# Expert layer: 0/1 products on TensorE turn slots into tokens; rows gathered and results scattered block by block

## The chip, the cores and the metric

The kernel runs on one core of a Trainium2 chip. The metric is device time in microseconds (us). A core has TensorE (matmuls), VectorE, ScalarE and GpSimd (called DVE, ACT and POOL in the profile), and SyncE (SP). SP and ACT issue plain DMAs, GpSimd the indirect ones, whose addresses come from a table in SBUF.

## The reference

A decoder of two layers on x [2, 1024, 256] (2048 tokens of 256 values). The change lies in the mixture of experts that ends the first layer:

```python
moe_in = _layer_norm(x_resid, ln2_g, ln2_b)
xf = moe_in.reshape(N, D)
probs = jax.nn.softmax(xf @ w_gate, axis=-1)
top_w, top_i = jax.lax.top_k(probs, TOP_K)
top_w = top_w / top_w.sum(-1, keepdims=True)
for e in range(E):
    gate_e = jnp.sum(jnp.where(top_i == e, top_w, 0.0), axis=-1)
    he = jax.nn.gelu(xf @ w1[e] + b1[e])
    out = out + gate_e[:, None] * (he @ w2[e] + b2[e])
return out.reshape(B, S, D) + x_resid
```

N is 2048 tokens, D 256, the hidden width F 1024, E 8 experts, TOP_K 2. Everything is float32.

## The kernel before

Stages follow each other, each a block of five instruction streams with a barrier between blocks: mixers, cross attention, self attention, `norm`, `experts`, and then the second layer. Activations stay in SBUF with the 256 features on partitions (h, res, x: 128 partitions x 2 x 2048 tokens).

`experts` doesn't run all tokens through all experts. Each token has two chosen experts, so there are 4096 (token, choice) pairs. They are sorted into slots: each expert owns whole blocks of NSL = 256 slots, and NB = 23 blocks hold any distribution (5888 slots).

**Routing.** SP loads seven small tables (L2118). TensorE makes the logits, 16 tiles of 128 tokens, 8 columns each (L2154), then transposes h into rows of tokens (L2161), which ScalarE copies to `ht` (L2360). VectorE takes the softmax and ranks the experts of a token by comparing all pairs (L2267 to L2271), TensorE counts ahead of each token (L2167, L2168), and VectorE turns the counts into `owner` (L2291: the expert of each block, which lets SP and ACT load the first weights, L2122 and L2353) and `place` (L2300: the slot of each token's choices).

**Dispatch.** GpSimd scatters the rows of `ht` to their slots in a DRAM tensor `moe_in_rows` that SP filled with zeros during the norm, 16 tiles x 2 choices (L2384). SP waits for all 32 and loads the first blocks of 256 rows (L2126).

**Loop over the blocks b.** TensorE turns a block's rows back to columns (`turn`, L2183), multiplies by w1 (`first`, L2194), ScalarE applies gelu (L2371), TensorE multiplies by w2 (`second`, L2206). VectorE copies the turned columns (`keep_columns`, L2314) and the results (`keep_rows`, L2321). SP loads rows and w1 two blocks ahead and stores results to `moe_out_rows` (L2132); ACT loads w2. The order on TensorE is written out by hand:

```python
for b in range(NB):
    if b + 1 < NB:
        first(b + 1)
    if b + 2 < NB:
        turn(b + 2)
    second(b)
```

**End.** GpSimd gathers each token's two result rows tile by tile into a ring of 8 (L2392). For each tile VectorE forms share0 x row0 + bias (L2336) and adds share1 x row1 (L2340), TensorE turns the sum (L2237), and after every fourth tile VectorE adds it to x (L2347). The bias products are TensorE's too (L2226). VectorE adds res to x beforehand (L2308).

## Time and profile before

| | us |
|---|---|
| median of 3 runs (2878.31 to 2885.4) | 2885.22 |
| the profiled execution, its own time | 2872.27 |
| its span | 2870.4 |
| TensorE busy in the span | 2411.5 (84%) |
| VectorE busy | 1872.3 (65%) |
| GpSimd busy | 1530.5 (53%) |
| ScalarE busy | 1301.5 (45%) |

The profile is one execution, with times from the start of its span. Busy shares are means over stages with different limits, so the part around the change has to be read by itself: `norm` ends at 1614.0 and the expert stage runs from there to 2090.3, about 476 us. The granted clock is TensorE's, as a share of 2.4 GHz; it has two levels, 0.5 (1.2 GHz) and 1.0. A float32 matmul stands as two records.

### The profile page before, as it was taken

How to read it: one execution, taken by the hardware profiler on the slowest of the kernel's cores; microseconds unless marked ns; L12 is line 12 of the kernel's file. 1: busy time of each engine (PE TensorE's matmuls, PEld its weight loads, DVE VectorE, ACT ScalarE, POOL GpSimd, SP SyncE). 2: the span in 40 equal slices, each digit the busy share in tenths (PEclk: the TensorE clock that was granted, in tenths of full speed). 3: DMA queues.
4: the chain of work that ended last, by engine and by line, in shares of the span. 5: the costliest groups of instructions: out<-in, count | busy, mean ns of one | idle time of the engine just before them, and what ended most of it. 6: DMA issues, size and time to landing. Idle time of an engine off the chain costs nothing. (4 is left out here: it accounts for less than half of the span.)

```text
span 2870.4 us, 26873 instructions
## 1 busy us (share of the span) xinstructions
PE 2411.5 (84%) x8432; PEld 1100.3 (38%) x8432; DVE 1872.3 (65%) x2521; ACT 1301.5 (45%) x2063; POOL 1530.5 (53%) x1340
## 2 busy tenths in 40 slices
PE   7989889899897778678888539999788899787868
PEld 3333323333332233333333328888533333223322
DVE  2999999999999933466653400000229999996334
ACT  4556566465664434345555202222045564543433
POOL 2999999999999811500000140000339999994110
PEclk9999999999999999899999669999789999999989
DMA  5031230312303000612310334444340312300000
GB/s 189 2 117 40 101 123 1 125 54 73 118 1 117 0 22 17 145 23 33 46 23 1 103 128 183 176 173 170 109 166 3 117 45 74 118 0 21 1 9 30
DMA packets 72484, 215.18 MB, mean 75 GB/s; under 512 B 14331, under 2 KB 39558, under 8 KB 53782
## 3 DMA queue, kind: packets, MB, share of 16 engines
q1 hardware_dynamic: 65668, 180.85, 19.4%
q10 hardware_dynamic: 3602, 24.22, 2.6%
q0 software_dynamic: 3072, 8.39, 0.9%
q8 instruction: 68, 1.11, 0.2%
q14 instruction: 74, 0.61, 0.1%
HBM read 187.80 MB, written 25.43 MB: 74 GB/s over the span
## 5 line engine op out<-in xcount | busy, mean ns | idle before, releaser
L897 POOL TENSOR_TENSOR s_dbu<-s_dx,s_bc 128x512 f32<-128x512 f32 x768 | 966.9, 1282 | 35.0 <-DVE s_psum L561 31.5
L480 PE MATMUL s_psum<-s_hc,ident 128*128 128x512 f32 x1536 | 834.6, 634 | 168.3 <-DVE s_hc L581 145.6
L764 ACT ACTIVATE s_psum<-s_dt,s_a_neg 128x512 f32<-128x512 f32 x768 | 521.6, 688 | 606.6 <-DVE s_hc L581 605.6
L480 PEld LDWEIGHTS s_psum<-s_hc,ident 128*128 128x128 f32 x1536 | 258.9, 193 | 684.6 <-DVE s_hc L581 479.5
L581 DVE TENSOR_TENSOR s_hc<-s_psum,s_bc 128x512 f32<-128x512 f32 x624 | 419.8, 673 | 0.6 <-PE s_psum L480 0.4
L561 DVE TENSOR_TENSOR_SCAN s_psum<-s_psum,s_state,s_dbu 128x512 f32<-128x512 f32 x312 | 395.2, 1278 | 10.9 <-POOL s_dbu L897 7.2
L561 DVE TENSOR_TENSOR_SCAN s_psum<-s_psum,s_dbu 128x512 f32<-128x512 f32 x312 | 381.3, 1222 | 14.3 <-POOL s_dbu L897 11.9
L1979 ACT ACTIVATE s_probs<-s_banks 128x512 f32<-128x512 f32 (+3 forms) x384 | 169.7, 493 | 148.6 <-PE s_banks L1704 105.8
L2392 POOL DMA_INDIRECT s_rows_in<-moe_out_rows,s_place x32 | 30.8, 963 | 358.5 <-DMA moe_out_rows<-s_ys 349.1
L2371 ACT ACTIVATE s_hidden<-s_banks,s_w 128x256 f32<-128x256 f32 x184 | 77.1, 470 | 302.5 <-PE s_banks L2194 302.5
L163 POOL TENSOR_TENSOR s_pair<-s_res 128x512 f32<-128x512 f32 x4 | 5.0, 1269 | 384.5 <-issue 383.1
L432 PE MATMUL s_psum<-s_pad,s_taps 128*128 128x512 f32 x384 | 191.2, 592 | 0.0
L908 POOL TENSOR_TENSOR s_hc<-s_hs,s_bc 128x512 f32<-128x512 f32 x144 | 182.8, 1269 | 15.4 <-DVE s_hs L561 15.4
L1828 DVE TENSOR_REDUCE s_umax<-s_banks 128x1 f32<-128x512 f32 (+3 forms) x256 | 138.8, 585 | 69.7 <-PE s_banks L1672 58.9
L2194 PE MATMUL s_banks<-s_xt,s_w 128*128 128x256 f32 x736 | 164.3, 382 | 0.0
L2206 PE MATMUL s_banks<-s_w,s_hidden 128*128 128x256 f32 x736 | 162.5, 379 | 0.0
L1669 PE MATMUL s_banks<-s_stack_k,s_stack_q 96*128 96x512 bf16 (+3 forms) x384 | 130.1, 347 | 34.2 <-DVE s_umax L1828 26.3
L1701 PE MATMUL s_banks<-s_stack_q,s_stack_k 99*128 99x512 bf16 (+3 forms) x384 | 130.0, 355 | 28.5 <-DMA s_stack_q<-s_row 23.5
L2314 DVE COPY s_xt<-s_banks 128x512 f32<-128x512 f32 x23 | 15.9, 691 | 205.2 <-PE s_banks L2183 205.2
L2194 PEld LDWEIGHTS s_banks<-s_xt,s_w 128*128 128x128 f32 x736 | 141.0, 192 | 19.8 <-DVE s_xt L2314 0.3
L2206 PEld LDWEIGHTS s_banks<-s_w,s_hidden 128*128 128x128 f32 x736 | 138.2, 190 | 17.9
L2321 DVE COPY s_ys<-s_banks 128x512 f32<-128x512 f32 x23 | 15.9, 691 | 149.9 <-PE s_banks L2206 149.9
(304 smaller groups left out, 3320.6 us busy)
## 6 DMA issues: line engine op xcount, KB each, us to landing
s_bc<-fwd_rows SPq DMA_DIRECT2D x64, 1024.0 KB, 4.7
s_bc<-m_rows SPq DMA_DIRECT2D x32, 1024.0 KB, 4.7
s_w<-in_moe_w SPq DMA_DIRECT2D x23, 1028.0 KB, 7.2
s_w<-in_moe_w ACTq DMA_DIRECT2D x23, 1024.0 KB, 5.5
qk_parts<-s_parts SPq DMA_DIRECT2D x48, 128.0 KB, 1.9
s_stack_q<-qk_parts SPq DMA_DIRECT2D x48, 128.0 KB, 4.5
s_stack_k<-qk_parts SPq DMA_DIRECT2D x48, 128.0 KB, 7.6
moe_in_rows<-s_zero SPq DMA_DIRECT2D x1, 5888.0 KB, 18.8
```

Source lines behind the costliest of these rows:

```text
L432: mm = pe.matmul(bank(w), taps[:, m * TAPS + j, :], pad[:, m, j:j + CH], start=(j == 0), stop=(j == TAPS - 1))
L480: pe.matmul(psum[:, SCANS + block_no % 2, :], consts["ident"][:], hc[:, unit % PRODUCTS, :], start=(n == 0), stop=(n == NS - 1)).then_inc( ...
L561: dve.tensor_tensor_scan(hs[:] if LENT[i] else h, h, dbu[:, unit % TERMS, :], begin, ALU.mult, ALU.add)\
L581: dve.tensor_tensor(hc[:, unit % PRODUCTS, :], psum[:, unit % SCANS, :], bc[:, 2 * n + 1, :], ALU.mult)\
L764: act.activation(psum[:, unit % SCANS, :], dt[:, g % 2, i // NS, :], ACT.Exp, scale=a_neg[CHUNKS[g][0]][:, i:i + 1]).then_inc(decay_ready, 1)
L897: pool.tensor_tensor(dbu[:, unit % TERMS, :], dx[:, g % 2, i // NS, :], bc[:, 2 * n, :], ALU.mult)\
L908: pool.tensor_tensor(hc[:, unit % PRODUCTS, :], hs[:], bc[:, 2 * (i % NS) + 1, :], ALU.mult)\
L1669: mm = pe.matmul(bank[:, 0:w], stack_q[0:STACK, q % SLOTS, j, t * P:(t + 1) * P], stack_k[0:STACK, q % SLOTS, j, half * CH:half * CH + w], ...
L1828: dve.tensor_reduce(to, banks[:, i % 2, 0:w], AX.X, ALU.max).then_inc(max_read, 1)
L1979: act.activation(probs[:, u % 2 * HH + j, 0:w], banks[:, WEIGHT_BANKS[i % len(WEIGHT_BANKS)], 0:w], ACT.Exp)\
L2194: mm = pe.matmul(up[:, f, :], w1[:, b % 2, k * F + f * P:k * F + (f + 1) * P], xt[:, b % 2, k, :], start=(k == 0), stop=(k == KD - 1))
L2206: mm = pe.matmul(down[:, b % 2, half * D:(half + 1) * D], hidden[:, b % 2, f, half * P:(half + 1) * P], w2[:, b % 2, f * D:(f + 1) * D], s ...
```

## The change

- The routing tables (nine now) are loaded during `norm`; the zeros and the tile they came from are gone.
- Logits: the gate is the stationary operand and 512 tokens stream past it, 4 x 2 matmuls into 8 partitions. ScalarE copies each chunk (L2392 of the new file) and TensorE transposes 16 tiles of it (L2157).
- Ranks: 14 smaller compares that write straight into a zeroed tile.
- Slots to tokens: each place is split into `high` (place / 128) and `low` (place mod 128). VectorE compares them with a row of numbers, giving 0/1 tiles `high_hot` and `low_hot` in bf16. ScalarE multiplies `high_hot` by the partition number, GpSimd by the tile number. 32 matmuls sum low_hot.T @ high_hot, which gives for each slot whether it is held, and by which token and choice. VectorE makes from it `token` (row to gather) and `target` (row to store to; empty slots get rows of their own past the 4096).
- Rows: SP stores `ht` plainly (L2137). GpSimd gathers each block's rows, two DMAs of 128 rows into one of XR = 3 buffers, and scatters its results, two DMAs (L2425, L2432 of the new file).
- End: results lie in order of (choice, token), so SP and ACT load them with four plain DMAs each. The ring is gone.
- `gate_t` is copied by ScalarE instead of VectorE, and x + res is taken in two halves inside the loop.

```diff
+        def load_results(engine, n):
+
+            for parity in range(2):
+                engine.wait_ge(ys_stored[parity], (NB + 1 - parity) // 2 * 32)
+            for c in range(NCH):
+                engine.dma_start(rows_in[:, n, 4 * c:4 * c + 4, :],
+                                 ys_d[n * T + c * CH:n * T + (c + 1) * CH, :].rearrange("(t p) d -> p t d", p=P))\
+                      .then_inc(rows_loaded[c], 16)
...
+            for c in range(NCH):
+                sp.wait_ge(ht_ready, 2 * c + 2)
+                sp.dma_start(ht_d[c * CH:(c + 1) * CH, :].rearrange("(t p) d -> p t d", p=P), ht[:, 4 * c:4 * c + 4, :])\
+                  .then_inc(ht_stored, 16)
...
-            sp.wait_ge(scattered, 2 * NT * 16)
-            for b in range(2):
-                load_rows(b)
-            for b in range(NB):
-                if b + 2 < NB:
-                    sp.wait_ge(xs_turned, b + 1)
-                    load_rows(b + 2)
-                    sp.wait_ge(hidden_ready, (b + 1) * FB)
-                    load_first(b + 2)
-                store_rows(b)
+            for b in range(NB - 2):
+                sp.wait_ge(hidden_ready, (b + 1) * FB)
+                load_first(b + 2)
+            load_results(sp, 0)
...
+            for c in range(NCH):
+                for k in range(KD):
+                    mm = pe.matmul(flat[:, c, :], w_gate[:, k, :], h[:, k, c * CH:(c + 1) * CH],
+                                   start=(k == 0), stop=(k == KD - 1))
+                mm.then_inc(logits_made, 1)
             for t in range(NT):
-                for k in range(KD):
-                    mm = pe.matmul(lg[:, t, :], h[:, k, t * P:(t + 1) * P], w_gate[:, k, :],
-                                   start=(k == 0), stop=(k == KD - 1))
+                pe.wait_ge(logits_kept, t // 4 + 1)
+                mm = pe.transpose(lg[:, t, :], gate_t[:, t * P:(t + 1) * P], consts["ident"][0:E, 0:E])
             mm.then_inc(logits_ready, 1)
...
+            for i in range(NP):
+                if i % 8 == 0:
+                    pe.wait_ge(low_ready, i // 8 + 1)
+                if i == 0:
+                    pe.wait_ge(high_done, 2)
+                mm = pe.matmul(held.rearrange("p v r -> p (v r)"), low_hot[:, i, :],
+                               high_hot[:, i, :, :].rearrange("p v r -> p (v r)"), start=(i == 0), stop=(i == NP - 1))
+            mm.then_inc(held_ready, 1)
             pe.wait_ge(gate_stored, 1)
...
-                pe.wait_ge(xs_loaded[b % 2], (b // 2 + 1) * 16)
+                pe.wait_ge(xs_loaded[b % XR], (b // XR + 1) * 32)
...
-            pairs = [pair_cmp[:, n].rearrange("p t (i j) -> p t i j", i=E) for n in range(2)]
-            other = prob.unsqueeze(2).to_broadcast([P, NT, E, E])
-            own = prob.unsqueeze(3).to_broadcast([P, NT, E, E])
-            dve.tensor_tensor(pairs[0], other, own, ALU.is_gt)
-            link(dve.tensor_tensor(pairs[1], other, own, ALU.is_equal))
-            link(dve.tensor_tensor(pairs[1], pairs[1], before[:].unsqueeze(1).to_broadcast([P, NT, E, E]), ALU.mult))
-            link(dve.tensor_tensor(pairs[0], pairs[0], pairs[1], ALU.add))
-            link(dve.tensor_reduce(rank, pairs[0], AX.X, ALU.add))
+            dve.wait_ge(loaded, len(routing) * 16)
+            for i in range(E):
+                own = prob[:, :, i:i + 1]
+                if i:
+                    last = dve.tensor_tensor(pair_cmp[:, :, i, 0:i], prob[:, :, 0:i], own.to_broadcast([P, NT, i]), ALU.is_ge)
+                if i + 1 < E:
+                    last = dve.tensor_tensor(pair_cmp[:, :, i, i + 1:E], prob[:, :, i + 1:E],
+                                             own.to_broadcast([P, NT, E - 1 - i]), ALU.is_gt)
+            link(last)
+            link(dve.tensor_reduce(rank, pair_cmp[:], AX.X, ALU.add))
...
+            places = place_f[:].rearrange("p n t -> p (n t)")
+            link(dve.tensor_scalar(high[:], places, 1.0 / P, 0.5 / P - 0.5, ALU.mult, ALU.add))
+            link(dve.tensor_scalar(high[:], high[:], 12582912.0, None, ALU.add))
+            link(dve.tensor_scalar(high[:], high[:], -12582912.0, None, ALU.add))
+            link(dve.scalar_tensor_tensor(out=low[:], in0=high[:], scalar=-float(P), in1=places, op0=ALU.mult, op1=ALU.add))
+            dve.tensor_tensor(high_hot[:, :, 0, :], iota[:, 0:NR].unsqueeze(1).to_broadcast([P, NP, NR]),
+                              high[:].unsqueeze(2).to_broadcast([P, NP, NR]), ALU.is_equal).then_inc(high_ready, 1)
+            for i in range(0, NP, 8):
+                dve.tensor_tensor(low_hot[:, i:i + 8, :], iota[:].unsqueeze(1).to_broadcast([P, 8, P]),
+                                  low[:, i:i + 8].unsqueeze(2).to_broadcast([P, 8, P]), ALU.is_equal).then_inc(low_ready, 1)
+            dve.wait_ge(held_ready, 1)
+            link(dve.tensor_copy(source[:], held[:, 1, :]))
+            link(dve.scalar_tensor_tensor(out=source[:], in0=held[:, 2, :], scalar=float(P), in1=source[:],
+                                          op0=ALU.mult, op1=ALU.add))
+            link(dve.tensor_scalar(shift[:], source[:], T - 0.5, -float(T), ALU.is_ge, ALU.mult))
+            link(dve.tensor_tensor(shift[:], shift[:], source[:], ALU.add))
+            dve.tensor_copy(token[:], shift[:]).then_inc(token_ready, 1)
+            link(dve.scalar_tensor_tensor(out=empty[:], in0=held[:, 0, :], scalar=0.5, in1=part[:, 1:1 + NR],
+                                          op0=ALU.is_lt, op1=ALU.mult))
+            link(dve.tensor_tensor(source[:], empty[:], source[:], ALU.add))
+            dve.tensor_copy(target[:], source[:]).then_inc(target_ready, 1)
...
-            dve.tensor_copy(gate_t[:], flat.rearrange("e c t -> e (c t)")).then_inc(gate_stored, 1)
-            dve.tensor_tensor(x[:], x[:], res[:], ALU.add).then_inc(summed, 1)
...
+                if 1 <= b <= KD:
+                    dve.tensor_tensor(x[:, b - 1, :], x[:, b - 1, :], res[:, b - 1, :], ALU.add).then_inc(summed, 1)
...
-                dve.wait_ge(gathered[t % RING], (t // RING + 1) * 32)
+                if t % 4 == 0:
+                    dve.wait_ge(rows_loaded[t // 4], 32)
...
+            act.activation(gate_t[:], flat.rearrange("e c t -> e (c t)"), ACT.Copy).then_inc(gate_stored, 1)
...
+            act.activation(high_hot[:, :, 1, :], high_hot[:, :, 0, :], ACT.Copy, scale=part[:, 0:1]).then_inc(high_done, 1)
...
-            pool.wait_ge(ht_ready, NT // 2)
-            pool.wait_ge(blank, 16)
-            for n in range(2):
-                pool.wait_ge(place_ready, n + 1)
-                for t in range(NT):
-                    pool.indirect_dma_start(out=xs_d, out_offset=bass.IndirectOffsetOnAxis(ap=place[:, n, t:t + 1], axis=0),
-                                            in_=ht[:, t, :], in_offset=None).then_inc(scattered, 16)
-            for b in (NB - 2, NB - 1):
-                pool.wait_ge(ys_stored[b % 2], (b // 2 + 1) * 16)
-            for t in range(NT):
-                if t >= RING:
-                    pool.wait_ge(y_ready, t - RING + 1)
-                for n in range(2):
-                    pool.indirect_dma_start(out=rows_in[:, t % RING, n, :], out_offset=None, in_=ys_d,
-                                            in_offset=bass.IndirectOffsetOnAxis(ap=place[:, n, t:t + 1], axis=0))\
-                        .then_inc(gathered[t % RING], 16)
+            def gather(b):
+                if b >= XR:
+                    pool.wait_ge(xs_turned, b - XR + 1)
+                for half in range(2):
+                    pool.indirect_dma_start(out=xs[:, b % XR, half, :], out_offset=None, in_=ht_d,
+                                            in_offset=bass.IndirectOffsetOnAxis(ap=token[:, 2 * b + half:2 * b + half + 1], axis=0))\
+                        .then_inc(xs_loaded[b % XR], 16)
+
+            def scatter(b):
+                pool.wait_ge(ys_ready, b + 1)
+                for half in range(2):
+                    pool.indirect_dma_start(out=ys_d,
+                                            out_offset=bass.IndirectOffsetOnAxis(ap=target[:, 2 * b + half:2 * b + half + 1], axis=0),
+                                            in_=ys[:, b % 2, half, :], in_offset=None).then_inc(ys_stored[b % 2], 16)
+
+            pool.wait_ge(high_ready, 1)
+            pool.tensor_tensor(high_hot[:, :, 2, :], high_hot[:, :, 0, :],
+                               iota[:, 0:NP].unsqueeze(2).to_broadcast([P, NP, NR]), ALU.mult).then_inc(high_done, 1)
+            pool.wait_ge(ht_stored, NCH * 16)
+            pool.wait_ge(token_ready, 1)
+            for b in range(XR):
+                gather(b)
+            pool.wait_ge(target_ready, 1)
+            for b in range(NB):
+                if b + XR < NB:
+                    gather(b + XR)
+                scatter(b)
...
-                     prefetch=[(rows_d.rearrange("(b p) d -> p b d", p=P),
-                                zero[:].unsqueeze(1).to_broadcast([P, NB * NSL // P, D]), blank)])
-                experts(core, consts, h, res, x, rows_d, blank)
+                     prefetch=[(t[:], dram["moe_" + key], loaded) for key, t in routing.items()])
+                experts(core, consts, h, res, x, routing, loaded)
```

Three places show what moves.

GpSimd, from the start of the expert stage; `s_xs` holds a block's gathered rows, `s_ys` its results. Before:

```order
L63 ISA x9
L2377 UNCONDITIONAL_BRANCH
L2384 DMA moe_in_rows<-s_ht,s_place 5888x256 x32
L2392 DMA s_rows_in<-moe_out_rows,s_place 128x256 x32
L56 UNCONDITIONAL_BRANCH
```

now (the alternation goes on to the last block):

```order
L2419 UNCONDITIONAL_BRANCH
L2437 TENSOR_TENSOR s_high_hot<-s_high_hot,s_iota 128x32x46
L2425 DMA s_xs<-moe_in_rows,s_token 128x256 x8
L2432 DMA moe_out_rows<-s_ys,s_target 9984x256 x2
L2425 DMA s_xs<-moe_in_rows,s_token 128x256 x2
L2432 DMA moe_out_rows<-s_ys,s_target 9984x256 x2
L2425 DMA s_xs<-moe_in_rows,s_token 128x256 x2
```

The 32 scatters ahead of the loop and the 32 gathers behind it give way to the gathers of blocks 0 to 3 (8 DMAs), then two scatters and two gathers in turn.

TensorE, from the start of the expert stage; `s_gate_t` is the copied logits, `s_low_hot` and `s_high_hot` are the 0/1 tiles. Before:

```order
L2149 UNCONDITIONAL_BRANCH
L2154 MATMUL s_banks<-s_w_gate,s_h 128x8 x32
L2161 MATMUL s_banks<-ident,s_h 128x128 x32
L2167 MATMUL s_banks<-s_small,s_ahead 128x128
L2168 MATMUL s_banks<-s_small,s_ahead 128x128
L2172 MATMUL s_banks<-ident,s_small 8x128 x16
L2183 MATMUL s_banks<-ident,s_xs 128x128 x8
L2194 MATMUL s_banks<-s_xt,s_w 128x256 x32
L2183 MATMUL s_banks<-ident,s_xs 128x128 x4
```

now:

```order
L2147 UNCONDITIONAL_BRANCH
L2152 MATMUL s_banks<-s_h,s_gate 8x512 x8
L2157 MATMUL s_banks<-ident,s_gate_t 128x8 x16
L2163 MATMUL s_banks<-ident,s_h 128x128 x32
L2169 MATMUL s_banks<-s_small,s_ahead 128x128
L2170 MATMUL s_banks<-s_small,s_ahead 128x128
L2174 MATMUL s_banks<-ident,s_small 8x128 x16
L2181 MATMUL s_banks<-s_high_hot,s_low_hot 128x138 x32
L2193 MATMUL s_banks<-ident,s_xs 128x128 x8
L2204 MATMUL s_banks<-s_xt,s_w 128x256 x32
L2193 MATMUL s_banks<-ident,s_xs 128x128 x4
```

The logits are 8 wide matmuls and 16 transposes instead of 32 narrow ones, and the 32 products stand ahead of the first turned rows.

SP, from the end of its small loads; `s_w` is a block's w1. Before:

```order
L2122 DMA s_w<-in_moe_w 128x2056
L2121 TENSOR_LOAD s_owner
L2121 ISA x2
L2122 ISA
L2122 DMA s_w<-in_moe_w 128x2056
L2126 DMA s_xs<-moe_in_rows 128x2x256 x3
L2121 TENSOR_LOAD s_owner
L2121 ISA x2
L2122 ISA
L2122 DMA s_w<-in_moe_w 128x2056
L2132 DMA moe_out_rows<-s_ys 128x2x256
```

now:

```order
L2128 UNCONDITIONAL_BRANCH
L2137 DMA moe_in_rows<-s_ht 128x4x256 x4
L2131 TENSOR_LOAD s_owner
L2131 ISA x2
L2132 ISA
L2132 DMA s_w<-in_moe_w 128x2056
L2131 TENSOR_LOAD s_owner
L2131 ISA x2
L2132 ISA
L2132 DMA s_w<-in_moe_w 128x2056
```

The row loads and result stores leave SP's list, so that only the weight loads stay in the loop.

## Rows read from the trace of the kernel before

**Rows 1.** Windows: length, busy PE, PEld, DVE, ACT, POOL, clock, DMA share, GB/s.
```profile
1614.00:1633.00 19.00, 13.67 (x64) 13.67 (x65) 0.00 (x0) 0.00 (x0) 0.00 (x0) 0.50 0.07 15
1702.37:2042.35 339.98, 334.09 (x1561) 288.17 (x1561) 31.10 (x45) 77.10 (x184) 0.00 (x0) 0.99 0.45 164
2045.00:2090.00 45.00, 22.88 (x56) 11.57 (x56) 19.78 (x36) 0.00 (x0) 30.83 (x32) 0.50 0.32 94
```

**Rows 2.** Routing timeline: start, us, engine, line, operation, [idle before, releaser].
```profile
1619.33 13.82 PE L2154 MATMUL s_banks<-s_w_gate,s_h 128*128 128x8 f32 x64 [15.21 <-DMA s_ahead<-in_moe_ahead]
...
1634.14 0.60 ACT L2360 ACTIVATE s_ht<-s_banks 128x512 f32<-128x512 f32 x1
...
1635.20 1.23 DVE L2267 TENSOR_TENSOR s_pair_cmp<-s_small 128x1024 f32<-128x1024 f32 x1
...
1640.11 1.22 DVE L2271 TENSOR_REDUCE s_small<-s_pair_cmp 128x128 f32<-128x1024 f32 x1
...
1642.78 2.77 PE L2172 MATMUL s_banks<-ident,s_small 128*8 128x128 f32 x16
...
1647.12 0.29 DVE L2299 TENSOR_REDUCE s_place_f<-s_small 128x16 f32<-128x128 f32 x1
```

**Rows 3.** Timeline of the dispatch.
```profile
1646.63 0.17 DVE L2300 CAST s_place<-s_place_f 128x16 int32<-128x16 f32 x1
...
1647.72 1.20 POOL L2384 DMA_INDIRECT moe_in_rows<-s_ht,s_place  x1 [44.78 <-DVE s_place L2300]
...
1649.23 7.03 POOL L2384 DMA_INDIRECT moe_in_rows<-s_ht,s_place  x1 [0.31 <-issue]
1651.01 4.40 DVE L2308 TENSOR_TENSOR x<-x,s_res 128x4096 f32<-128x4096 f32 x1
...
1697.56 4.41 SPq L2126 DMA_DIRECT2D s_xs<-moe_in_rows  x3
...
1700.50 1.94 PE L2183 MATMUL s_banks<-ident,s_xs 128*128 128x128 f32 x8 [54.95 <-DMA s_xs<-moe_in_rows]
...
1702.37 15.87 PE L2194 MATMUL s_banks<-s_xt,s_w 128*128 128x256 f32 x64
```

**Rows 4.** Timeline of the end.
```profile
2041.66 0.69 DVE L2321 COPY s_ys<-s_banks 128x512 f32<-128x512 f32 x1 [6.22 <-PE s_banks L2206]
2045.23 0.99 POOL L2392 DMA_INDIRECT s_rows_in<-moe_out_rows,s_place  x1 [349.10 <-DMA moe_out_rows<-s_ys]
...
2049.31 0.48 DVE L2336 SCALAR_TENSOR_TENSOR s_half_y<-s_rows_in,s_share,s_banks 128x256 f32<-128x256 f32 x1 [6.96 <-DMA s_rows_in<-moe_out_rows,s_place]
...
2050.37 0.69 PE L2237 MATMUL s_banks<-ident,s_y 128*128 128x128 f32 x2 [6.83 <-DVE s_y L2340]
...
2053.43 2.07 PE L2226 MATMUL s_banks<-s_b,s_gate_t 8*128 8x256 f32 x4
...
2089.04 1.22 DVE L2347 TENSOR_TENSOR x<-x,s_banks 128x1024 f32<-128x1024 f32 x1 [0.78 <-PE s_banks L2237]
```

**Rows 5.** Timeline of the next stage's first matmuls.
```profile
2090.59 5.93 PE L402 MATMUL s_psum<-x,ones 128*128 128x512 f32 x8 [1.58 <-PEq L56]
...
2101.42 7.13 PE L422 MATMUL s_psum<-s_xn,s_w_in 128*128 128x512 f32 x16 [0.98 <-DVE s_xn L599]
```

**Rows 6.** GpSimd by line: duration ns min/median/max; timeline beside VectorE.
```profile
L2009 POOL TENSOR_TENSOR s_parts<-s_rest,s_parts x16: 1151/1154/1164, 1151.6 to 1204.7; 128x512 bf16<-128x512 f32 x16
...
L841 POOL TENSOR_SCALAR s_w_in<-s_w_in,norms x12: 1552/1564/2306, 15.6 to 2102.8; 128x512 f32<-128x512 f32 x12
...
2100.14 1.23 DVE L599 TENSOR_TENSOR s_xn<-s_res,s_gate 128x1024 f32<-128x1024 f32 x1 [2.37 <-ACT s_gate L671]
2100.49 3.85 POOL L841 TENSOR_SCALAR s_w_in<-s_w_in,norms 128x512 f32<-128x512 f32 x2 [2.25 <-DMA s_w_in<-in_m_in]
```

**Rows 7.** DMA issues, 1646 to 1700: KB each, median us to landing.
```profile
s_w<-in_moe_w SPq DMA_DIRECT2D x2, 1028.0 KB, 10.0
```

**Rows 8.** Waits, 1702 to 2045: us in total, times, longest.
```profile
PE s_banks L2183 <- DMA s_xs<-moe_in_rows: 5.6, 17, 0.6
```

More of the change, by code:

```diff
@@ L2039, with experts @@
 W2ROW = FB * D
-RING = 8
-def experts(core, consts, h, res, x, xs_d, blank):
+NR = NB * NSL // P
+XR = 3
+def experts(core, consts, h, res, x, routing, loaded):
     dram = core.dram
@@ L2050, in experts @@
         NT = B * QT
-        w_gate = s.sb("w_gate", [P, KD, E])
-        b2 = s.sb("b2", [E, D])
-        before = s.sb("before", [P, E, E])
-        again = s.sb("again", [P, E * NT])
-        sizes = s.sb("sizes", [P, E])
-        order = s.sb("order", [P, NB])
-        ahead = s.sb("ahead", [P, 2, P])
+        NP = 2 * NT
+        w_gate, b2, before, again, sizes, order, ahead, iota, part = (
+            routing[key] for key in ("gate", "b2", "before", "again", "sizes", "order", "ahead", "iota", "part"))
         w1 = s.sb("w1", [P, 2, W1ROW])
@@ L2071, in experts @@
         place_f = s.sb("place_f", [P, 2, NT])
-        place = s.sb("place", [P, 2, NT], mybir.dt.int32)
+        high, low = s.sb("high", [P, NP]), s.sb("low", [P, NP])
+        low_hot = s.sb("low_hot", [P, NP, P], BF16)
+        high_hot = s.sb("high_hot", [P, NP, 3, NR], BF16)
+        source, empty, shift = s.sb("source", [P, NR]), s.sb("empty", [P, NR]), s.sb("shift", [P, NR])
+        token = s.sb("token", [P, NR], mybir.dt.int32)
+        target = s.sb("target", [P, NR], mybir.dt.int32)
         share = s.sb("share", [P, 2, NT])
@@ L2106, in experts @@
         down_ready, ys_ready = s.sem("down_ready"), s.sem("ys_ready")
[L2107 removed]
+        rows_loaded = [s.sem(f"rows_loaded{c}") for c in range(NCH)]
         bias_ready, half_ready, y_ready, y_turned, added = (s.sem("bias_ready"), s.sem("half_ready"), s.sem("y_ready"),
@@ L2111, in experts @@
         block = s.block()
-        LOADS = ((w_gate, "moe_gate"), (b2, "moe_b2"), (before, "moe_before"), (again, "moe_again"),
-                 (sizes, "moe_sizes"), (order, "moe_order"), (ahead, "moe_ahead"))
+        def load_results(engine, n):
[5 more added lines that the diff above has]
+                      .then_inc(rows_loaded[c], 16)
         @block.sync
         def _(sp):
-            for t, key in LOADS:
-                sp.dma_start(t[:], dram[key]).then_inc(loaded, 16)
             def load_first(b):
@@ L2254, in wide @@
                 return v.to_broadcast([P, NT, E])
+            dve.memset(pair_cmp[:], 0.0)
             dve.wait_ge(logits_ready, 1)
@@ L2354, in load_second @@
                   .then_inc(w2_loaded[b % 2], 16)
+            for c in range(NCH):
+                act.wait_ge(logits_made, c + 1)
+                act.activation(gate_t[:, c * CH:(c + 1) * CH], flat[:, c, :], ACT.Copy).then_inc(logits_kept, 1)
             act.wait_ge(step, 2)
@@ L2725, in program @@
                 h = s.sb("h", [P, KD, T])
-                zero = s.sb("zero", [P, D])
-                self_attention(core, consts, x, h, res, lns, zero)
-                blank = s.sem("blank")
-                rows_d = nc.dram_tensor("moe_in_rows", (NB * NSL, D), F32, kind="Internal").ap()
+                self_attention(core, consts, x, h, res, lns)
+                loaded = s.sem("loaded")
+                routing = {key: s.sb(key, dram["moe_" + key].shape)
+                           for key in ("gate", "b2", "before", "again", "sizes", "order", "ahead", "iota", "part")}
                 norm(core, consts, res, h, True, weight=lns[:, 2, :], bias=lns[:, 3, :],
-                     prefetch=[(rows_d.rearrange("(b p) d -> p b d", p=P),
-                                zero[:].unsqueeze(1).to_broadcast([P, NB * NSL // P, D]), blank)])
-                experts(core, consts, h, res, x, rows_d, blank)
+                     prefetch=[(t[:], dram["moe_" + key], loaded) for key, t in routing.items()])
+                experts(core, consts, h, res, x, routing, loaded)
         if 3 in stages:
```

56 lines of the change are left out of this document (28 added, 28 removed).

## The prediction

> **What bounds the kernel now.** I read the windows by stage first, then the timeline of the expert stage, then the waits. In the windows [rows 1] the reader should see three different stages. The logits run TensorE for 13.67 of 19.0 us at a granted clock of 0.50. The block loop keeps it busy for 334.09 of 339.98 us at 0.99. The combination at the end keeps it busy for half of its 45 us, with GpSimd busiest at 30.83. So the loop is bound by TensorE, and time can be won only in front of it and behind it. In the timeline of the routing [rows 2] VectorE runs a chain of small steps and TensorE's first matmul waits for the last of seven small loads. In the timeline of the dispatch [rows 3] GpSimd issues 32 scatters one behind another from 1647.72 on, SP fetches the first rows at 1697.56, and TensorE stands for 54.95 us until they are back. At the end [rows 4] GpSimd issues 32 gathers and VectorE takes up each tile as it lands.
>
> The sum below is made against the profiled execution, 2872.27 us (span 2870.4). The median of the three runs shown is 2885.22, which is 12.95 more. The gain is taken off both, and the forecast is for the median.
>
> **The change, part by part.** Times are those of the trace before.
>
> *Routing loads.* Nine loads are issued in the norm in place of the 5.9 MB of zeros. They have over 20 us to land, and nothing else uses the DMAs there: free. TensorE can start about 0.3 after the stage begins at 1614.0 [rows 1], as the next stage's first matmul does (2090.59 after the last addition's end at 2090.26 [rows 4, 5]), instead of at 1619.33 [rows 2]: **-5.0**. The dropped zeros and memset are worth nothing, since nothing waited for them.
>
> *Logits.* 64 records with 8 columns each took 13.82 us [rows 2]. They become 8 matmuls of 512 columns, 16 records. Such records after an idle TensorE took 5.93 us for the first 8, and at the full clock 7.13 us for 16, so 0.45 each [rows 5]. That gives 5.93 + 8 x 0.45 = 9.5 us. If the clock stayed at 0.50, as it did for the 8-column matmuls, it would be some 13.7, and if it rose sooner, 8. Behind them come ScalarE's copy of the last chunk (0.60 [rows 2]) and four transposes of 8 rows (0.17 each by the nearest row, 2.77 us for 16 [rows 2]), with the hand-overs about 1.4. I take 10.5 to 10.9 against 13.86: **-3.2** (bounds -4.5 and +1.2).
>
> *Ranks.* Four passes of 1024 elements, 1635.20 to 1640.11, become 14 compares over 16 to 112 elements, 896 in all. At 1.23 us per 1024 elements that is 1.1, plus some 0.07 of overhead for each: 2.1. **-2.8** (bounds -3.5 and -1.5).
>
> *From places to tokens.* The places are complete at 1647.12 + 0.29 = 1647.4, shifted by the 11.0 above to 1636.4. New and on the path: four steps of 32 elements (0.2 each, as the 16-element cast of 0.17 [rows 3] with its link), the high compare over 1472 elements (1.23 x 1472/1024 = 1.8), then on GpSimd a product over 1472 elements. GpSimd took 1.154 us for 512 with a bf16 result [rows 6], so 3.3. TensorE waits for it and then runs 32 matmuls of 138 columns at the lower clock: 138 columns at 1.2 GHz are 0.115 us, and 16 transposes took 2.77, 0.17 each [rows 2]; between them, 4.5. Then five small steps on VectorE, 1.1, and 0.9 to the first DMA, as between the cast's end at 1646.80 and the first scatter at 1647.72 [rows 3]. ScalarE's product (under 2 us) and its two weight loads lie beside GpSimd's.
>
> One thing is open: VectorE meanwhile runs four low compares of 1024 elements, 1.2 each and back to back, both operands in SBUF. A row bears on it. GpSimd's scaling of 512 elements takes 1.56, but the one that began at 2100.49 took 2.31, while VectorE multiplied two SBUF tiles until 2101.37 [rows 6]. So it lost 0.75 of 0.88 us of overlap. I therefore let GpSimd's product start only when the four compares are done, 4.7 after the high compare. With free overlap the path is 4.7 shorter.
>
> The Trainium skill says the same more strictly (SBUF — State Buffer, "Who interferes with whom"): a VectorE instruction with two SBUF inputs and a GpSimd instruction that reads SBUF exclude each other for a whole instruction. By that rule the sum is as I take it; were the ports free, it would be 4.7 lower.
>
> Sum: 1636.4 + 0.8 + 1.8 + 4.7 + 3.3 + 4.5 + 1.1 + 0.9 = 1653.5 for the first gather's issue. By then the weights, loaded from some 1635 on beside 2 MB of stored rows, should have landed: in the trace before, four such loads had landed 10.0 us after their issue [rows 7].
>
> *Dispatch.* 32 scatters, their landing and the loads back are replaced by four gathers ahead of the first matmul. GpSimd's indirect DMAs take 0.96 (30.83 us for 32 at the end [rows 1]) and 0.30 between them, so they follow each other in 1.26, and a pair is usable 4.08 after its first issue (2045.23 to 2049.31 [rows 4]). Block 1's rows are there 2.5 later, at 1653.5 + 6.6 = 1660.1, and with 0.9 of transposes (1700.50 to 1702.37 for two blocks) the first expert matmul starts at 1661.0 instead of 1702.37 [rows 3]: **-41.4**, which includes the 11.0 above. Free overlap would make it -46.1; one gather held as the second scatter was (7.03 [rows 3]) would make it -35.6.
>
> *Loop.* TensorE's 17 waits for block rows, 5.6 us [rows 8], should go: the rows of block b+3 are asked for three half-blocks (21 us) ahead, with three buffers. **-5.0** (bounds 0 and -5.6). GpSimd takes four DMAs a block, 4 x 1.26 = 5.0 us of a block's 14.75 ((2041.66 - 1702.37)/23). SP, relieved of two transfers, issues w1 earlier: free. The residual add moves into the loop, 2 x 2.2 us (half of 4.40 [rows 3]) ahead of two copies of results; a half-block of TensorE work of 7 us covers it, and without that cover it costs 4.4.
>
> *End.* VectorE's last copy starts at 2041.66 and ends at 2042.35; the end comes with the last addition, 2089.04 + 1.22 = 2090.26 [rows 4], 47.9 later. Now: second scatter issued 1.4 after the copy, landed 2.6 later (4.0), then eight plain loads of 512 KB on two queues. The nearest row is the load of block rows, issued at 1697.56 and in use at 1700.50 [rows 3]: 2.9 for some 0.5 MB, so 4.6 for the first pair. That is 8.6 before the first tile. From there TensorE paces at its lower clock [rows 4]: four tiles cost 4 x 0.69 for their transposes and two bias pairs of 2.07, 6.9, with the wait at the addition 7.3, so 29.2 for 16. Sum 37.8: **-10.1**. Were VectorE the pace (4 x 1.02 for two passes of 0.48 and their hand-overs, 0.78 of waiting, 1.22 for the addition: 6.1) it would be -14.9. Were all 4 MB needed first it would be -3.
>
> Total -41.4 - 5.0 - 10.1 = **-56.5**: 2872.27 becomes 2815.8, the median 2885.22 becomes **2828.7**.
>
> **The order** confirms it: GpSimd's list now alternates two gathers and two scatters; behind a scatter that waits for its results stands only the gather of three blocks later.
>
> **Rivals.** The trace before has no indirect DMA beside the loop's weight traffic. The nearest is the second scatter, 7.03 us instead of 0.96, begun at 1649.23 while four weight loads were in flight [rows 3]. VectorE's long addition from 1651.01 ended at 1655.42, so the trace alone doesn't tell which of the two held it.
>
> 1. *GpSimd's queue fills partly.* If two of a block's four DMAs take 7.03, a block needs 2 x 7.03 + 2 x 1.26 = 16.6, 1.8 over TensorE's 14.75; 23 blocks give back 42, and the 5 of the loop are lost: 2885.2 - 51.5 + 42 = 2876. For it: the row. Against: two loads of 1 MB now start a half-block apart rather than together.
> 2. *Slower: GpSimd becomes the bound.* If three of four take 7.03, a block needs 22.4, 7.6 over: +175, 3009. It decides from (56.5 - 5)/23 = 2.2 over 14.75, that is 17.0 a block or 4.2 per DMA. Against: 30 of 32 scatters and all gathers went at 1.26, beside little other traffic.
> 3. *The change doesn't shorten the front and end as drawn*: one of the first gathers waits 7.03 behind the weights (5.8), and the plain loads are needed whole (7): -43.8, 2841.
>
> **How the numbers follow.** Forecast 0.74, rival 1 0.09, rival 2 0.05, rival 3 0.12. The unknowns inside the forecast (overlap 4.7 and logits 1.3 down; logits 4.4, loop 5 and gather 5.8 up; end 4.8 down and 7 up; not all at once) give it 2808 to 2843. As the median stands 13 above the profiled run, a lower base counts too; the range of 8 in 10 is 2804 to 2847, and leaves out rivals 1 and 2. A measurement of this kernel tells about 0.3% (8.7 us) from no change. Rival 1 just misses that band, at -9, so I give 0.03 to "same" from it, 0.05 to slower and 0.92 to faster.
>
> **What would show it.** Right: the first expert matmul some 47 us after the norm's end (88 before); GpSimd's product starting only after the low compares; no TensorE wait for xs in the loop; GpSimd's DMAs in the loop near 1 us; 38 us from the last copy to the last addition. Wrong: indirect DMAs of 4 us or more on average in the loop, TensorE waiting for xs or VectorE for stored rows, or a granted clock still at 0.50 at the end of the logits.

## The result and the profile after

| us | median | lowest to highest | runs |
|---|---|---|---|
| before | 2885.31 | 2878.31 to 2890.64 | 4 |
| changed | 2807.20 | 2803.45 to 2809.56 | 4 |

The ratio is 0.9731 (95% interval 0.9719 to 0.9744): 78.1 us less. A later set of runs beside the kernel before gave 0.9766 (0.9752 to 0.9779), 2808.44 against 2877.18, 68.7 us less. The forecast was 2828.7, with a range of 2804 to 2847. The profiled execution took 2809.56, its span is 2807.5 (2870.4 before).

I cut each trace at four marks: the end of the norm (VectorE's last operation there), TensorE's first expert matmul, the end of VectorE's last copy of results, and the end of the last addition to x. "Stage" is the sum of front, loop and end; "after it" is the rest of the span.

| us | norm ends | front | loop | end | stage | after it |
|---|---|---|---|---|---|---|
| before | 1614.0 | 88.4 | 340.0 | 47.9 | 476.3 | 780.1 |
| changed | 1616.7 | 44.1 | 329.2 | 36.0 | 409.4 | 781.4 |
| difference | +2.7 | -44.3 | -10.8 | -11.9 | -66.9 | +1.2 |

The windows of the changed kernel, which answer to [rows 1]: length, busy PE, PEld, DVE, ACT, POOL, clock, DMA share, GB/s.

```profile
1616.73:1628.02 11.29, 10.97 (x33) 2.81 (x34) 0.92 (x2) 2.34 (x4) 0.00 (x0) 0.73 0.00 1
1660.86:1989.40 328.54, 328.54 (x1558) 288.79 (x1557) 34.83 (x46) 77.11 (x184) 81.56 (x83) 1.00 0.51 169
1990.00:2025.00 35.00, 23.31 (x62) 12.77 (x61) 17.97 (x37) 0.00 (x0) 1.94 (x2) 0.57 0.40 128
```

In the loop TensorE is now busy for all of the 328.54 us, and GpSimd has 81.56 us of work there, where it had none. The timeline of the front, which answers to [rows 2, 3]:

```profile
1617.05 9.85 PE L2152 MATMUL s_banks<-s_h,s_gate 128*8 128x512 f32 x16 [10.16 <-PEq L56]
...
1628.02 0.29 DVE L2270 TENSOR_REDUCE s_col<-s_banks 128x16 f32<-128x128 f32 x1 [9.81 <-PE s_banks L2157]
...
1638.89 0.29 DVE L2313 TENSOR_REDUCE s_place_f<-s_small 128x16 f32<-128x128 f32 x1
...
1641.70 7.08 DVE L2322 TENSOR_TENSOR s_low_hot<-s_iota,s_low 128x1024 bf16<-128x1024 f32 x4
...
1641.86 3.57 POOL L2437 TENSOR_TENSOR s_high_hot<-s_high_hot,s_iota 128x1472 bf16<-128x1472 bf16 x1 [36.15 <-DVE s_high_hot L2319]
...
1645.57 4.37 PE L2181 MATMUL s_banks<-s_high_hot,s_low_hot 128*128 128x138 bf16 x32 [8.93 <-POOL s_high_hot L2437]
...
1652.00 1.18 POOL L2425 DMA_INDIRECT s_xs<-moe_in_rows,s_token  x1 [6.57 <-DVE s_token L2330]
...
1656.42 1.08 PE L2193 MATMUL s_banks<-ident,s_xs 128*128 128x128 f32 x4 [6.49 <-DMA s_xs<-moe_in_rows,s_token]
1659.95 1.11 PE L2193 MATMUL s_banks<-ident,s_xs 128*128 128x128 f32 x4 [2.44 <-DMA s_xs<-moe_in_rows,s_token]
```

The reader should see that GpSimd's product starts 0.08 after the high compare (1641.78) instead of behind the four low compares, and that these take 7.08 us together. The timeline of the end, which answers to [rows 4, 5]:

```profile
1989.40 0.69 DVE L2352 COPY s_ys<-s_banks 128x512 f32<-128x512 f32 x1 [6.22 <-PE s_banks L2218]
1990.37 0.97 POOL L2432 DMA_INDIRECT moe_out_rows<-s_ys,s_target  x1 [4.23 <-DVE s_ys L2352]
1991.65 0.97 POOL L2432 DMA_INDIRECT moe_out_rows<-s_ys,s_target  x1 [0.31 <-issue]
1994.08 2.72 SPq L2124 DMA_DIRECT2D s_rows_in<-moe_out_rows  x4
...
1999.76 0.48 DVE L2370 SCALAR_TENSOR_TENSOR s_half_y<-s_rows_in,s_share,s_banks 128x256 f32<-128x256 f32 x1 [9.67 <-DMA s_rows_in<-moe_out_rows]
...
2005.51 1.22 DVE L2381 TENSOR_TENSOR x<-x,s_banks 128x1024 f32<-128x1024 f32 x1 [2.00 <-PE s_banks L2249]
2006.64 0.47 DVE L2370 SCALAR_TENSOR_TENSOR s_half_y<-s_rows_in,s_share,s_banks 128x256 f32<-128x256 f32 x1
...
2024.90 1.22 DVE L2381 TENSOR_TENSOR x<-x,s_banks 128x1024 f32<-128x1024 f32 x1 [0.78 <-PE s_banks L2249]
...
2026.45 6.60 PE L402 MATMUL s_psum<-x,ones 128*128 128x512 f32 x8 [1.58 <-PEq L56]
```

### The profile page after: what moved, and what is told of

Read it like the earlier page. It is cut to its first block and busy times, and to the rows that moved or that the text cites. A ratio compares the mean times of both kernels' runs of the same rounds, so it can differ in the third digit from the quotient of the medians.

```text
span 2807.5 us, 26907 instructions
## 1 busy us (share of the span) xinstructions
PE 2407.8 (86%) x8432; PEld 1092.6 (39%) x8432; DVE 1878.5 (67%) x2547; ACT 1307.1 (47%) x2069; POOL 1556.0 (55%) x1368
## 5 line engine op out<-in xcount | busy, mean ns | idle before, releaser
L2432 POOL DMA_INDIRECT moe_out_rows<-s_ys,s_target x46 | 45.5, 989 | 236.5 <-DVE s_ys L2352 229.5
L422 PE MATMUL s_psum<-s_xn,s_w_in 128*128 128x512 f32 x192 | 101.7, 636 | 15.2 <-ACT s_pad L691 10.7
```

## The experiments

"Before" and "changed" name the two kernels. Front, loop, end and stage are the marks' columns above, in us.

**The kernel before, again.** No edit.

> The kernel before, unchanged, to see where one execution of it spends more than another. Its profiled execution took 2872.27 us, its median 2885.31. Theory: the 13 us lie in the expert stage, in the 64 indirect DMAs that GpSimd issues with nothing else running, so the stage (476.3 us in the first trace) is up to 13 us longer here while the mixers keep their time. Rival: they lie in the mixers, where the change touches nothing, and the expert stage is again 476 within 2 us. Either way the ratio to the kernel before is 1.000.

Measured: 2883.78 of 10 runs, ratio 1.0002 (0.9992 to 1.0011). Front 88.4 and loop 340.3 repeat to 0.3 us. The end doesn't: 54.6 instead of 47.9, and the norm ends at 1626.5. So neither expectation holds alone: of the 20.2 us by which this span is longer, 12.5 lie ahead of the expert stage and 7.0 in it. The timeline of VectorE in its end shows two pauses, while GpSimd went on issuing gathers at 1.26:

```profile
2085.20 0.48 DVE L2340 SCALAR_TENSOR_TENSOR s_y<-s_rows_in,s_share,s_half_y 128x256 f32<-128x256 f32 x1
2092.37 0.48 DVE L2336 SCALAR_TENSOR_TENSOR s_half_y<-s_rows_in,s_share,s_banks 128x256 f32<-128x256 f32 x1 [6.68 <-issue]
...
2093.80 0.48 DVE L2340 SCALAR_TENSOR_TENSOR s_y<-s_rows_in,s_share,s_half_y 128x256 f32<-128x256 f32 x1
2102.92 1.22 DVE L2347 TENSOR_TENSOR x<-x,s_banks 128x1024 f32<-128x1024 f32 x1 [8.64 <-DMA s_bc<-fwd_rows]
```

All four later traces of this kernel and of its variants have an end of 54.6 to 54.8. They show two or three pauses of 3 to 9 us each, not always at the same tiles. The trace that the prediction was made from is the exception, by 6.8 us. What VectorE waits for in the pauses isn't shown ("issue", and a transfer of another stage), and no run here settled it.

**Before, with rows loaded three blocks ahead.**

```diff
-        xs = s.sb("xs", [P, 2, 2, D])
+        xs = s.sb("xs", [P, 3, 2, D])
...
-            for b in range(2):
+            for b in range(3):
                 load_rows(b)
```

> The kernel before with a third buffer for block rows, each plain load asked for three blocks ahead instead of two. Theory: the 10.7 us that the loop lost in the change (339.98 to 329.23) were TensorE's waits for rows which SP could only ask for behind the store of the block before, so a block goes from 14.75 to 14.25 us here too: 10 to 11 us faster. Rival: they came from w1, w2 and rows landing in one burst, which stays as it is here; then the block stays at 14.6 to 14.75 and the gain is under 3 us.

Measured: ratio 0.9967 (0.9955 to 0.998); the loop falls from 340.3 to 329.7, the changed kernel's 329.2. So the loop's gain is the third buffer's: plain loads get it as well. The timeline of TensorE in one block, first in the trace before (the two transposes' groups and the products between them):

```profile
1769.42 7.07 PE L2194 MATMUL s_banks<-s_xt,s_w 128*128 128x256 f32 x32
1776.85 0.66 PE L2183 MATMUL s_banks<-ident,s_xs 128*128 128x128 f32 x4 [0.35 <-DMA s_xs<-moe_in_rows]
1777.34 7.07 PE L2206 MATMUL s_banks<-s_w,s_hidden 128*128 128x256 f32 x32
```

and with three buffers:

```profile
1770.99 7.07 PE L2195 MATMUL s_banks<-s_xt,s_w 128*128 128x256 f32 x32
1777.89 0.60 PE L2184 MATMUL s_banks<-ident,s_xs 128*128 128x128 f32 x4
1778.33 7.07 PE L2207 MATMUL s_banks<-s_w,s_hidden 128*128 128x256 f32 x32
```

From one group's start to the next but one it is 7.92 and 7.34 us. The wait is shown as 0.35 but costs 0.58: the modelled ends of back-to-back matmul groups overlap the next group by 0.17, which an idle time leaves out, and the transposes after a wait take 0.05 more.

**The changed kernel with two buffers.** `XR = 2` instead of 3.

> The changed kernel with two buffers for gathered rows instead of three. GpSimd then asks for block b+2 once block b is turned, behind the two scatters of a block, so the rows have less than half a block to come. Theory (the loop's gain of 10.8 us comes from rows asked for early enough): four indirect DMAs of 1.26 plus 2.7 for the landing and the hand-over are 8.4 us against 7.1 us of TensorE work, so some 1.3 us a block for 22 blocks: loop 329 to about 358, time 2807 to about 2836. Rival (the gain comes from TensorE no longer sharing the DMA engines with SP's row loads, and the third buffer is a luxury): loop stays within 2 us of 329, time within 0.3%.

Measured: ratio 0.9892 (0.9867 to 0.9917), 2846.57; loop 364.7, 35.5 above the changed kernel. The waits of 15 blocks:

```profile
PEld s_banks L2193 <- DMA s_xs<-moe_in_rows,s_token: 28.1, 15, 3.0
PE s_banks L2193 <- DMA s_xs<-moe_in_rows,s_token: 22.1, 15, 2.6
```

The theory holds; its 1.3 us a block were 1.6. That it came so near is luck, since its sum has a slip: 4 x 1.26 + 2.7 is 7.7, not 8.4, and would give 0.6 a block. What it had too small is the way of a pair, which is usable 4.1 to 6.0 us after its first issue here (4.8 in the mean of 20 blocks). The third buffer is worth half of the change's gain: without it the gathers behind the scatters are late.

**Before, with the new logits and ranks** (tables loaded in the norm, 512 tokens per logits matmul, small compares).

> The kernel before with three parts of the change: tables loaded in the norm, wide logits with transposes, ranks by 14 small compares. Everything behind them as before. Theory: they give what their stretches show in the trace of the changed kernel, 5.0 + 2.9 + 2.9 = 10.8 us, and the rest of the kernel keeps its time. Rival: the scatters behind them start earlier but meet the weights or another limit, and less than 8 us arrives at the end.

Measured: ratio 0.9962 (0.9948 to 0.9976), front 76.5, 11.9 less. These terms of the sum (-11.0) stand.

**Before, with the residual sum in the loop.**

```diff
-            dve.tensor_tensor(x[:], x[:], res[:], ALU.add).then_inc(summed, 1)
...
+                if 1 <= b <= KD:
+                    dve.tensor_tensor(x[:, b - 1, :], x[:, b - 1, :], res[:, b - 1, :], ALU.add).then_inc(summed, 1)
```

> The kernel before with x + res moved into the loop, in two halves, as the change has it. It tells what held the second scatter for 7.03 us. Theory: the four weight loads, with the DMA engines fully busy; the scatter takes about 7 us again and the time stays within 0.1%. Rival: VectorE's addition of 4.40 us; then the scatter takes 1 to 3 us, the scatters end some 5 us earlier, and the kernel is about 5 us faster.

Measured: ratio 0.9985 (0.9975 to 0.9995), front 82.3, 6.1 less, as the rival had it. The second scatter, in the timeline of GpSimd in the kernel before run again:

```profile
1661.68 7.04 POOL L2384 DMA_INDIRECT moe_in_rows<-s_ht,s_place  x1 [0.30 <-issue]
...
1663.47 4.40 DVE L2308 TENSOR_TENSOR x<-x,s_res 128x4096 f32<-128x4096 f32 x1
```

and with the sum moved:

```profile
1653.17 2.28 DVE L2307 COPY s_gate_t<-s_banks 8x2048 f32<-8x2048 f32 x1
1653.59 0.97 POOL L2385 DMA_INDIRECT moe_in_rows<-s_ht,s_place  x1 [0.30 <-issue]
```

The four weight loads are in flight in both. So the 7.03 us on which rivals 1 and 2 rested were VectorE's long addition, not weight traffic.

**The changed kernel, low compares held back** until ScalarE's and GpSimd's products are done.

> The changed kernel with VectorE's four low compares made to wait until GpSimd's and ScalarE's products are done. In the changed kernel the four compares took 7.08 us, against some 4.6 for 4 x 1.15. Theory (GpSimd took the shared port first and VectorE stood for it): after the wait the four take 4.5 to 4.8 us back to back, the chain gets about 1.1 us longer up to the product matmuls' end (3.6 of waiting in place of 2.5 of standing). Rival (such compares with a bf16 result and broadcast operands cost 1.77 each by themselves): they take 7.0 to 7.1 again, and the chain gets 3.6 us longer.

Measured (one run, 2808.18): front 43.0, stage 409.1. GpSimd's product alone, then the compares alone:

```profile
1641.49 2.66 POOL L2438 TENSOR_TENSOR s_high_hot<-s_high_hot,s_iota 128x1472 bf16<-128x1472 bf16 x1 [34.79 <-DVE s_high_hot L2319]
1644.18 4.63 DVE L2323 TENSOR_TENSOR s_low_hot<-s_iota,s_low 128x1024 bf16<-128x1024 f32 x4 [2.77 <-POOL s_high_hot L2438]
```

Alone they take 2.66 and 4.63, 7.29 in all; side by side they take 7.08. They hardly overlap. From the high compare's end to the end of the product matmuls it is 8.6 us (1641.40 to 1649.97) and 8.2 in the changed kernel, so running them one after the other costs 0.4 us, not the 1.1 expected. (The front is 1.2 shorter all the same, because the logits took 8.50 us here and 9.85 there; see the last run.)

**The changed kernel, GpSimd's product held back** until the first low compare is done.

> The changed kernel with GpSimd's product made to wait for the first of VectorE's four low compares, so that it becomes ready while VectorE streams compares back to back. Theory as in the prediction (whoever streams keeps the port): GpSimd's product of 3.57 us is held until the last compare has ended and shows as about 7 us or starts late, the product matmuls start some 2.5 to 3.5 us later than in the changed kernel. Rival (the port changes hands at each instruction's end, so GpSimd gets in between the first and second compare or the next): product 3.6 to 4.8 us, VectorE's compares together again about 7 us, matmuls about 1.3 us later.

Measured (one run, 2809.84): product 3.57 again, from 1643.65. The compares by line: shortest, median and longest in ns.

```profile
L2322 DVE TENSOR_TENSOR s_low_hot<-s_iota,s_low x4: 1211/1216/3676, 1642.4 to 1648.2; 128x1024 bf16<-128x1024 f32 x4
```

Three compares take 1.21 and one 3.68, which is the length of the product longer. The product itself takes 0.91 more than its 2.66 alone, so the records show that the two exclude each other, not which waited first. The rival holds: GpSimd gets in between two compares, the matmuls start 1.2 us later (4.9 after the high compare's end instead of 3.8), and a stream of compares doesn't keep GpSimd out. From the high compare's end to the first gather it is 10.8 us here (1642.43 to 1653.27) and 10.2 in the changed kernel.

**Block 1 turned later, last loads cut.**

```diff
-            turn(1)
-            first(0)
+            first(0, between=1)
...
+TILES_OF = (0, 1, 2, 4, 8, 12, 16)
```

> The changed kernel with two edits and no new work: TensorE turns block 0, begins the products of block 0 and turns block 1 among them (in the changed kernel it stood 2.44 us for block 1's rows before any product), and the last stage's loads are cut so that the first tile's rows come in a DMA of their own (parts of 1, 1, 2, 4, 4, 4 tiles instead of 4 x 4). Theory (both stretches are waits on the path): norm's end to first product 44.2 to about 41.0 us, though the first block may give back 0.5; last copy to first addition 9.7 to about 6.7 us; together 5 to 6.5 us, ratio to the kernel before about 0.971. Rival (the first tile's rows land no earlier because the DMA engines serve all parts in turn, and block 1's products wait for its turned rows instead): less than 2 us.

Measured: 2804.74, ratio 0.9726 (0.9713 to 0.974), which the changed kernel's 0.9731 (0.9719 to 0.9744) doesn't differ from; stage 406.8. The front gives 2.5 and the loop takes back 1.8, because block 0 now runs longer at the lower clock (24 records in 8.09 us; at the full clock 32 take 7.07). The first tile is there 2.9 earlier, but VectorE then stands 2.12 for the third. So 0.7 of the 2.5 is left in front and 1.9 of the 2.9 at the end, 2.6 us in all for the 5 to 6.5 expected. Another trace of the changed kernel, without any edit, has a stage of 406.9 (last run), so this gain is read from the two waits and isn't shown in the time.

**TensorE kept at work in its pauses**, by matmuls that nobody reads.

> The changed kernel with TensorE matmuls on idle banks that nobody reads, put where TensorE stands before short work: 15 at the end of the norm, 13 before the slot products, 8 before the first rows are turned, 17 before the last stage's tiles. They compute nothing that is used. Theory (logits, first block and the end run at the 1.2 GHz level only because TensorE stood idle ahead): logits 9.85 to about 6.9 us, first block's 64 records 15.4 to about 13.8, groups of four tiles at the end from 6.87 to between 6.1 and 6.9, next stage's first 8 records 6.6 to about 3.5, together 6 to 11 us. Rival (the clock falls again as soon as the short work with its gaps begins): under 3 us, and the granted clock at the end stays 0.50.

Measured (one run, 2809.68): logits 7.03, slot products 2.14 instead of 4.37 (they start later, when most compares are done), but the added matmuls overran, the end rose to 38.7 and the stage to 411.8: nothing of the 6 to 11 us arrives. In the end the granted clock is 1.00 while the first four tiles are turned (2004 to 2008) and 0.50 from 2009 on, so it fell after four tiles, not after two as the next expectation says.

**The same with smaller numbers, and one more matmul per tile of the end.**

> The run with idle-bank matmuls again, their number cut so that none delays real work (11, 10, 7 and 10, each 0.87 us as that run showed, where its 15, 13, 8 and 17 overran by 2.4, 1.3 and 3.8 us), and one more of 256 columns behind each of the 16 tiles of the end. They compute nothing that is used. Theory (the clock fell back to 1.2 GHz after two tiles of the end because TensorE then stood too often, and the added matmuls keep it up): groups of four tiles at VectorE's pace, about 6.1 us instead of 6.87, next stage's first 8 records 6.6 to about 3.5, logits 9.85 to about 7; the stage 409.4 to about 401. Rival (the clock falls all the same): the added 16 matmuls cost 0.87 each at the lower clock, groups rise to about 10.3 us, the stage takes some 417.

Measured (one run, 2796.59): stage 403.1, end 33.3. The window over two groups of the end, and the next stage's first matmuls (6.60 in the changed kernel):

```profile
1998.00:2012.00 14.00, 11.94 (x54) 7.25 (x52) 11.24 (x21) 0.00 (x0) 0.00 (x0) 1.00 0.25 78
...
2016.99 3.67 PE L406 MATMUL s_psum<-x,ones 128*128 128x512 f32 x8 [1.15 <-PEq L56]
```

The granted clock is 1.00 instead of 0.50. A group of four tiles takes 6.09 instead of 6.87 us: VectorE's pace, 6.1, as the prediction's other value for the end had it.

**All of it together.**

> The changed kernel with what the runs before showed to pay: block 1 turned among the products of block 0, the last loads cut into parts of 2, 2, 4, 4, 4 tiles, and matmuls on idle banks in TensorE's pauses (11, 10, 7 and 8 of 512 columns, and one of 256 columns for each tile of the end), which compute nothing that is used. Theory (the parts add up, since they lie in different stretches): from the 403.0 us of the stage with idle-bank matmuls, 2.4 less in front (block 1's rows no longer waited for, now at the full clock, so that the early start isn't given back) and 1.7 less at the end: stage 399, next stage 3 shorter, time about 2793, ratio to the kernel before 0.968. Rival (the idle-bank matmuls overrun where the real work now comes earlier, and the cut loads stall VectorE at the third tile again): stage 402 to 405, time 2797 or more.

Measured: 2798.74, ratio 0.9726 (0.9712 to 0.9739), stage 397.8 (front 37.8, loop 328.4, end 31.6). The stage came as the theory had it, the time didn't (2793 expected): it was reckoned from a single run whose norm ended at 1613.6, and here the norm ends at 1623.5, ahead of the stage.

**The changed kernel, again**, because the kernel before took 2885 in some sets of runs and 2877 in others.

> The changed kernel as it is, timed again beside the kernel before. The combined version took 2798.7 us where the kernel before took 2877.5, and the changed kernel 2807.2 where the kernel before took 2885.3, so the two ratios don't differ. Theory (the combined version's stage, 397.9 us against 409.4, is a real gain, and the ratio found for the changed kernel was a low one): the ratio is 0.975 to 0.977 this time, and the expert stage 409 to 410 us. Rival (the combined version loses elsewhere what it gains in the stage): ratio 0.973 again with a stage of 409 to 410.

Measured: 2808.44, ratio 0.9766 (0.9752 to 0.9779), stage 406.9, front 42.2. The ratio is in the range expected, the stage 2.5 us shorter than in the first trace with no edit at all. The timeline of TensorE shows where most of it comes from, the same 16 records of the logits and the slot products (9.85 and 4.37 in the first trace):

```profile
1616.80 8.49 PE L2152 MATMUL s_banks<-s_h,s_gate 128*8 128x512 f32 x16 [10.15 <-PEq L56]
...
1643.96 3.93 PE L2181 MATMUL s_banks<-s_high_hot,s_low_hot 128*128 128x138 bf16 x32 [8.92 <-POOL s_high_hot L2437]
```

The granted clock is 1.00 from the fifth of the 16 records on here and from the eighth in the first trace, so a difference of 1 to 2 us between two fronts, each from one trace, says nothing of an edit. Beside a kernel before of the same speed, 2877.5 and 2877.2, the combined version is 0.4% faster than the changed kernel, and the intervals don't touch. Its slowest run (2801.38) is also below the fastest of the changed kernel in either set (2803.45), and its stage is 9.1 us shorter. Only the single run with matmuls on idle banks alone, 2796.59, is lower.

## Why the prediction held, and where it didn't

The direction and the place of the gain were right, the size too small: 56.5 forecast, 78.1 measured (68.7 in the later set). That 2807.2 lies inside the range, 3 us above its lower end, is owed to the width of the range: front, loop and end were all forecast too small, by 10.4 together, and the rest of the miss lies outside the stage. The stage of the profiled executions gave 66.9. Of the 11.2 that remain, 6.8 would be the kernel before's usual end of 54.6, which its profiled execution did without; the last 4.4 were not traced further (the norm's end alone moves between 1613.6 and 1626.5 from one execution to the next). This split isn't shown: beside the later set's kernel before, 8 us faster with nothing changed, only 1.8 would remain. The prediction saw that the median stood 13 above its trace and took it for a constant; if the split is right, part of it was a cost that the change removes.

**Front, -44.3 for -41.4.** The start (0.3 after the norm), the logits (10.97 for 10.5 to 10.9), the ranks (2.04 for 2.1) and the places' end (22.5 us after the norm's end for 22.4) came as worked out. *From places to tokens* took 12.8 for 17.1. The step that failed is "I therefore let GpSimd's product start only when the four compares are done": it started 0.08 us after the high compare instead of 4.7, and the record of VectorE's first compare is 2.46 us longer instead, a time in which TensorE was waiting for the product anyway. The row for it [rows 6], a GpSimd operation that lost 0.75 of 0.88 us, said that the two exclude each other, not that a later compare would go ahead of the product. By the Trainium skill (SBUF — State Buffer, "Who interferes with whom") "Issue order, not op shape, decides who blocks". By that sentence a product issued behind the first compare waits for that one and not for three more, so the prediction's "By that rule the sum is as I take it" didn't follow from it. The trace agrees in that: the product lost 0.91, less than one compare. The exclusion agrees with 7.08 against 7.29 alone; which of the first two is held isn't settled, as compare 1 was issued 0.16 ahead of the product and ended with it. From the first gather to the first product it took 8.9 for 7.5: a pair was usable after 4.4 and the second pair 3.5 behind the first. This partly made up for the 4.3 gained before it.

**Loop, -10.8 for -5.0,** outside the bounds of 0 and -5.6. The mechanism was right, and the run with three buffers alone shows it (-10.6). The term was mis-sized: *"TensorE's 17 waits for block rows, 5.6 us"* counted the matmul row alone, and the row of its weight loads, in the same view of the trace before, says more:

```profile
PEld s_banks L2183 <- DMA s_xs<-moe_in_rows: 13.9, 20, 1.0
PE s_banks L2183 <- DMA s_xs<-moe_in_rows: 5.6, 17, 0.6
```

The truth, 10.6, lies between the two. It is read safely from starts: 14.83 us from one block's transposes to the next's in the middle of the loop (14.5 to 15.1 over the blocks behind the first) against 14.25.

**End, -11.9 for -10.1.** The first tile came after 9.7 for 8.6. The pace was 6.87 a group for 7.3, with TensorE as the bound as forecast (VectorE waits 2.00 for it at each addition but the last, where it is 0.78). Total 36.0 for 37.8.

**Rivals.** 1 and 2 needed indirect DMAs of 4 us or more beside the weights. The groups by line show none (shortest, median and longest in ns):

```profile
L2425 POOL DMA_INDIRECT s_xs<-moe_in_rows,s_token x46: 942/962/1178, 1652.0 to 1945.0; - x46
...
L2432 POOL DMA_INDIRECT moe_out_rows<-s_ys,s_target x46: 969/988/1012, 1684.6 to 1991.6; - x46
```

With three buffers TensorE has no wait for rows at all, so the Trainium skill's rule on queues served in turn (DMA: Bandwidth & Descriptors, "Queues, rings and completion order") cost nothing on the path here. It isn't refuted: a pair's way took 4.1 us in the quiet end of the kernel before and 4.1 to 6.0 in the loop with two buffers. Rival 3's late loads are real in part: one DMA for four tiles keeps the first waiting, 9.7 against 6.8 when it comes alone.

## What to carry to other kernels

Take the cost of a recurring wait from the distance between starts, with and without it, not from the idle time of one row. When transfers get a longer way (GpSimd's list, two gathers behind two scatters), a buffer more is part of the change: here it was worth 35.5 us of the loop. Before a slow DMA is put down to traffic, look for a long two-input VectorE operation beside it.

## What the runs showed of the hardware

- A VectorE addition of two SBUF tiles, 4.40 us, made an indirect scatter take 7.04 instead of 0.97 us (7.03 or 7.04 in all four traces that have the addition there), though it is recorded as starting 1.8 us after the scatter. How a scatter that should have been issued by then is caught isn't shown.
- GpSimd's product and VectorE's compares with two SBUF operands: 7.08 us side by side, 7.29 one after the other. One compare of four shows 3.68 instead of 1.21, and the product 3.57 instead of 2.66.
- In the end of the kernel before, VectorE pauses two or three times, for 3 to 9 us each, with nothing of its own stage shown to wait for, in four traces of five; the end has no such pause in any of the nine traces of the changed kernel and its variants.
- 16 matmuls of 256 columns that nobody reads, one per tile behind 10 of 512 columns, kept the granted clock at 1.00 in a stretch where TensorE had been busy 22 of 25 us at 0.50 without them; with them it was busy 11.94 of 14. With 17 of 512 columns ahead and none per tile the clock fell to 0.50 after four of the 16 tiles.
